# Start of a gated cross-attention kernel: second root sooner, VectorE scaling, x turned among V's products, K's first products in place of six warming ones

## What is computed

```python
h = _layernorm(x)                                 # over the 512 columns
x1 = h * rsqrt(mean(h * h) + EPS) * ln_weight
q, k, v = x1 @ w_q.T, ctx @ w_k.T, ctx @ w_v.T    # 32 heads of 128
score = softmax(where(m, q @ k + position_bias, -inf))
x = x + tanh(g_xattn) * (h + (score @ v) @ w_out.T)
x = x + tanh(g_ffn) * ffn(_layernorm(x))          # 28 experts of rank 8, the best 2
```

## Time and profile before

| | before |
|---|---|
| median of 3 runs | 825.04 us (824.33 to 826.55) |
| the profiled execution | 824.99 us, span 823.2 us |
| PE | 812.8 us busy (99%) |
| DVE | 592.9 us (72%) |
| ACT | 389.3 us (47%) |
| POOL | 454.0 us (55%) |
| mean granted clock | 0.998 |

### The profile page before, as it was taken

One profiled execution on the slowest core, in us unless ns is written; L12 is line 12 of the kernel. 1 busy time (PEld: TensorE's weight loads), 2 busy tenths in 40 slices (PEclk: granted clock), 3 DMA queues, 4 the chain that ended last, 5 costly groups with the idle time before them and its releaser, 6 DMA issues.

```text
span 823.2 us, 14190 instructions
## 1 busy us (share of the span) xinstructions
PE 812.8 (99%) x4198; PEld 694.3 (84%) x4198; DVE 592.9 (72%) x1003; ACT 389.3 (47%) x1059; POOL 454.0 (55%) x418
## 2 busy tenths in 40 slices
PE   9979999999999999999999999999999999999998
PEld 8868888887878888888888888888888888888887
DVE  6796556766775445996888778877887788778752
ACT  6954444445222424565445634563555355545410
POOL 2465666666388383757754575457545754574200
PEclk9999999999999999999999999999999999999999
DMA  9457545454543835797566556655665565555002
GB/s 319 142 182 254 174 155 165 153 162 158 179 179 116 293 129 179 236 259 264 161 211 227 180 165 213 219 180 165 219 210 182 166 226 207 179 184 179 1 27 77
DMA packets 79102, 149.70 MB, mean 182 GB/s; under 512 B 8032, under 2 KB 42336, under 8 KB 77024
## 3 DMA queue, kind: packets, MB, share of 16 engines
q1 hardware_dynamic: 79072, 149.32, 54.4%
HBM read 97.91 MB, written 51.38 MB: 181 GB/s over the span
## 4 chain that ended last, share of the span: by engine, by line
PE 91%; DVE 4%; ACT 2%; POOL 1%; DMA 1%; issue 1%; SPq 0%; DVEq 0%; POOLq 0%; ACTq 0%
PE proj_ps L2075 18%; PE proj_ps L1895 13%; PE proj_ps L2137 11%; PE proj_ps L2156 8%; PE score_ps L1895 6%; PE proj_ps L1945 5%; PE score_ps L2156 4%; PE score_ps L1914 3%; PE proj_ps L2341 2%; PE pv_ps L2137 2%; PE turn_ps L2137 2%; PE pv_ps L2156 2%; PE turn_ps L2156 2%; PE pv_ps L1914 2%; PE turn_ps L1914 2%; PE score_ps L1945 1%
## 5 line engine op out<-in xcount | busy, mean ns | idle before, releaser
L664 POOL TENSOR_TENSOR comb<-mask_add,bias_sb 128x1024 f32<-128x1024 f32 x32 | 78.3, 2468 | 145.1 <-DVE attn L1642 145.1
L906 ACT ACTIVATE attn<-attn,neg_max 128x128 f32<-128x128 f32 x256 | 99.2, 390 | 37.8 <-DVE neg_max L1631 37.7
L1161 ACT ACTIVATE w_hi<-w_raw 128x256 fp32r<-128x256 f32 x105 | 40.0, 413 | 100.1 <-POOL w_raw L755 75.2
L765 POOL TENSOR_TENSOR w_lo<-w_raw,w_hi 128x256 fp32r<-128x256 f32 x105 | 74.4, 751 | 1.8 <-ACT w_hi L1161 1.8
L1664 DVE TENSOR_TENSOR acc<-proj_ps,acc 128x512 f32<-128x512 f32 x70 | 48.1, 689 | 35.6 <-PE proj_ps L1895 35.6
L717 POOL TENSOR_TENSOR w_lo<-w_raw,w_hi 128x256 fp32r<-128x256 f32 x64 | 49.9, 783 | 25.1 <-ACT w_hi L1021 24.9
L1895 PE MATMUL proj_ps<-w_hi,tf_hi 128*128 128x512 f32 x156 | 61.1, 392 | 0.0
L1895 PE MATMUL proj_ps<-w_hi,tf_lo 128*128 128x512 f32 x156 | 60.7, 389 | 0.0
L1895 PE MATMUL proj_ps<-w_lo,tf_hi 128*128 128x512 f32 x156 | 60.7, 389 | 0.0
L660 POOL TENSOR_TENSOR w_lo<-w_raw,w_hi 128x1024 fp32r<-128x1024 f32 x19 | 45.7, 2410 | 16.1 <-ACT w_hi L892 16.1
L1457 DVE TENSOR_TENSOR w_lo<-w_raw,w_hi 128x256 fp32r<-128x256 f32 x48 | 35.2, 738 | 24.5 <-ACT w_hi L1016 24.1
(11 more groups left out here) (414 smaller groups left out, 2526.9 us busy)
## 6 DMA issues: line engine op xcount, KB each, us to landing
w_raw<-in_weights SPq DMA_DIRECT2D x50, 512.0 KB, 5.6
q_spill<-attn SPq DMA_DIRECT2D x64, 256.0 KB, 3.1
qt<-q_spill SPq DMA_DIRECT2D x16, 1024.0 KB, 4.8
v_sb<-v_spill SPq DMA_DIRECT2D x32, 512.0 KB, 3.8
block_spill<-block_sb SPq DMA_DIRECT2D x30, 512.0 KB, 3.5
attn<-block_spill SPq DMA_DIRECT2D x120, 128.0 KB, 3.0
w_raw<-in_v_weights SPq DMA_DIRECT2D x18, 512.0 KB, 4.4
v_spill<-v_sb SPq DMA_DIRECT2D x16, 512.0 KB, 4.8
```

The lines of the kernel that those rows point to most:

```text
L664: pool.tensor_tensor(comb[:, j, :, :], mask_add[:, :, :], bias_sb[:, j:j + 1, :].to_broadcast([P, B, S]), ALU.add).then_inc(comb_done, 1)
L765: pool.tensor_tensor(columns(w_lo, slot, n), raw, columns(w_hi, slot, n).bitcast(F32), ALU.subtract).then_inc(k_lo, 1)
L906: e = act.activation(probs[:, u, i, :], probs[:, u, i, :], ACT.Exp, bias=neg_max[:, u, i:i + 1], accum_out=row_sum[:, u, i:i + 1])
```

## The change

Seven places are edited. GpSimd makes the second inverse root ahead of the remainder of V's third block, and VectorE its variances ahead of the second half of the context's remainders. The layer norm of sequences 4 to 7 is applied by VectorE (a tensor_scalar with root and shift) instead of ScalarE. TensorE turns x's tiles 4 and 5 after two tiles of V's third block, and 6 and 7 after the other two. The six warming products behind the waits are gone, and K's first products stand there. In ScalarE's and VectorE's queues the splits of A, S and T are put in another order; t_raw[2] goes behind two remainders of A and two of T. GpSimd's first sums for Q's second phase wait for the third T remainder instead of Q's first product. The first context remainder moves behind Q's phases, and in V's group 1 a form is built before the last sums of group 0.

```diff
@@ gpsimd
             inverse_root(1, slice(0, G), 2)
-            pool.wait_ge(shift_done, 1)
+            inverse_root(2, slice(G, B), 2)
             early_rest(2)
-            inverse_root(2, slice(G, B), 2)
             pool.wait_ge(shift_done, 2)
             early_rest(3)
...
                 if isinstance(i, int) and i == 0:
-                    pool.wait_ge(q_prod, 1)
+                    pool.wait_ge(t_lo_done, 3)
...
-            pool.wait_ge(kt_hi_done, 1)
-            pool.tensor_tensor(kt_form_at(1, 0), kt_raw[0], kt_form_at(0, 0).bitcast(F32), ALU.subtract).then_inc(kt_lo_done, 1)
             q_phase(NQ - 2)
...
                 pool.tensor_tensor(v_raw(g, R21), v_raw(g, R22), v_raw(g, R11), ALU.subtract).then_inc(v_sums, 1)
                 if g < VE:
+                    v_last_sums(g - 1)
+                if g < VE:
                     pool.wait_ge(vw_in[R12], 16 * (g + 1))
...
+            rest_kt(0, 1)
             rest_kt(1, 2)
...
                 v_rest(g, 1)
-                v_last_sums(g - 1)
+                if g >= VE:
+                    v_last_sums(g - 1)
@@ scalar
-            layer(4)
-            layer(5)
+            raw_xt(0)
+            raw_xt(1)
             early_copy(2, 0)
-            raw_xt(0)
-            layer(6)
-            raw_xt(1)
-            early_copy(2, 1)
-            layer(7)
             raw_xt(2)
             raw_xt(3)
+            early_copy(2, 1)
+            lead_xt(4)
+            lead_xt(5)
             early_copy(2, 2)
             early_copy(2, 3)
-            lead_xt(4)
-            lead_xt(5)
...
             lead_a(0, 0, 0, 0)
+            lead_xt(6)
+            lead_xt(7)
+            early_copy(3, 0)
+            early_copy(3, 1)
+            lead_t(0)
+            lead_s(0, 0)
+            lead_s(0, 1)
+            lead_s(0, 3)
+            lead_s(0, 2)
             lead_a(0, 1, 0, 1)
             lead_a(0, 2, 1, 1)
-            lead_xt(6)
-            act.wait_ge(ve_prod, 2 * VTILES)
-            lead_s(0, 0)
-            lead_xt(7)
-            lead_t(0)
-            lead_s(0, 1)
-            early_copy(3, 0)
-            early_copy(3, 1)
             lead_t(1)
-            lead_s(0, 3)
-            lead_s(0, 2)
-            act.wait_ge(proj_done, UNITS)
             lead_t(3)
             early_copy(3, 2)
             early_copy(3, 3)
-            act.wait_ge(ve_prod, 4 * VTILES)
             lead_t(2)
@@ vector
             layer_shift(1, first)
+            x_variances(1)
             rest_ctx(0, 1)
             rest_ctx(1, 1)
             dve.wait_ge(small_in, 48)
             norm_x(0)
-            norm_x(1)
             rest_ctx(2, 1)
             rest_ctx(3, 1)
-            norm_x(2)
-            norm_x(3)
-            x_variances(1)
             layer_shift(2, second)
-            for i in range(G):
+            for i in range(1, G):
+                norm_x(i)
+            dve.wait_ge(shift_done, 2)
+            for i in range(G, B):
+                dve.tensor_scalar(acc[:, i, :], acc[:, i, :], root[:, 0, i:i + 1], shift[:, i:i + 1], ALU.mult, ALU.add).then_inc(acc_done, 1)
+            for i in range(0, G, 2):
                 rest_xt(i, xt_hi_done, xt_lo_done, xn_ps)
-            for i in range(G, B):
-                norm_x(i)
+                rest_xt(i + 1, xt_hi_done, xt_lo_done, xn_ps)
+                norm_x(G + i)
+                norm_x(G + i + 1)
...
             rest_a(0, 0, 0, 0)
-            rest_a(0, 1, 0, 1)
-            rest_a(0, 2, 1, 1)
...
             dve.tensor_tensor(t_raw[3], xt_raw[:, 2:4, half(0)], t_raw[1], ALU.subtract).then_inc(t_done, 1)
-            dve.tensor_tensor(t_raw[2], t_raw[1], xt_raw[:, 0:2, half(0)], ALU.subtract).then_inc(t_done, 1)
+            rest_a(0, 1, 0, 1)
+            rest_a(0, 2, 1, 1)
             rest_t(3, 3)
             rest_t(1, 2)
+            dve.tensor_tensor(t_raw[2], t_raw[1], xt_raw[:, 0:2, half(0)], ALU.subtract).then_inc(t_done, 1)
@@ tensor
-            pe.wait_ge(wk_part_in[0], 16)
-            for _ in range(4):
-                pe.matmul(score_ps[0][:, 0:P], ident[:, :], ident[:, :], start=True, stop=True)
-            pe.wait_ge(wk_part_lo, 1)
-            for _ in range(2):
-                pe.matmul(score_ps[0][:, 0:P], ident[:, :], ident[:, :], start=True, stop=True)
             first_keys(0)
...
-            for m in range(VTILES):
-                early_tile(2, m)
+            early_tile(2, 0)
+            early_tile(2, 1)
             turn_xn(4)
             turn_xn(5)
-            pe.wait_ge(ve_lo, 3)
-            early_tile(3, 0)
+            early_tile(2, 2)
+            early_tile(2, 3)
             turn_xn(6)
             turn_xn(7)
-            for m in range(1, VTILES):
+            pe.wait_ge(ve_lo, 3)
+            for m in range(VTILES):
                 early_tile(3, m)
```

More of the change, by code:

```diff
@@ L967, in layer @@
             def layer(i):
-                act.wait_ge(shift_done, i // G + 1)
+                act.wait_ge(shift_done, 1)
                 act.activation(acc[:, i, :], acc[:, i, :], ACT.Identity, bias=shift[:, i:i + 1], scale=root[:, 0, i:i + 1]).then_inc(acc_done, 1)
```

## The result

The changed kernel takes 827.75 us (median of 8 runs, 826.94 to 829.79) against 825.29 us before (8 runs, 824.33 to 826.55, same chip): a ratio of 1.003, 95% interval 1.0018 to 1.0042, or 2.5 us more. The forecast was 828.4, with 825.0 to 831.0 as range.

What follows compares the result with a forecast made beforehand. TensorE's waits were taken as the bound, Q's third product hanging on VectorE's queue. Terms: 4.8 at Q's third product, -1.1 near 237, -0.3 near 192, sum +3.4 on 825.04, so 828.4 us; range 825.0 to 831.0.

Steps and rivals of the forecast that it cites:

- TensorE passes K's second half unbroken: Sign against the forecast: no TensorE wait in K's second half, where about 2 us was expected at its third piece.
- What bounds the kernel: TensorE's waits are paid in full; at Q's start the third product hangs on VectorE's t_raw[2], through ScalarE's lead and copy.
- The start: K's first half, warming products removed: ends at 12.5 instead of 13.2, 0.7 us gained that buys nothing by itself.
- The second root: Root ahead of GpSimd's remainder: second shift 2.6 us sooner, but port waits and a new 2.0 us wait in K.
- A norm waits for GpSimd: VectorE's norm_x, reading two SBUF tiles, waits for GpSimd's remainder of V; taken as 2.2 us, bounds 0 and 2.2.
- the root holds no port: Rival: GpSimd's root does not block VectorE, so rest_ctx(1) and all behind come 1.5 us sooner; 827.1 us, chance 0.20.
- wait of 2.0 us at K's third piece: In K's second half, TensorE's third piece waits for rest_ctx(2) and starts at 28.4 instead of 26.2.
- The scaling: VectorE's four tensor_scalar replace ScalarE's layer(): 0.42 us each, 1.4 in all; T's first difference at 40.5 instead of 39.63.
- x among V's products: ScalarE copies V's tiles (3,0) and (3,1) before lead_t(0), so rest_t(0) starts at 46.3 instead of 45.17, +1.1 us.
- T's order: VectorE's queue before Q: two rest_a, rest_t(3) and rest_t(1) ahead of t_raw[2] make it +4.0 us later, ending at 54.9.
- The clock: Rival: clock falls after waits at 26 to 33 us and stays low longer at Q; 829.9 to 831, chance 0.13.
- Later: Form ahead of last sums near 237 gives -1.1 us; context remainder moved behind Q's phases, near 192, gives -0.3.

Runs made afterwards that it cites:

- e1_t2_back: Changed kernel with t_raw[2] again directly behind t_raw[3] in VectorE's queue; 824.32 us against 825.0 for the kernel before.
- e10_scalar_swap: Changed kernel with ScalarE's lead_t(2) behind the copies of Q's first two products; 824.28 us against 825.03 for the kernel before.
- e2_no_warming_alone: Kernel before without the six warming products, nothing else; 824.78 us against 825.0.
- e6_second_root_alone: Kernel before with only the second root and its variances sooner, second shift behind the context's remainders, ScalarE still scaling; 826.99 us against 825.75.
- e12_root_and_scaling: Kernel before with both the sooner second root and VectorE's scaling, nothing else of the change; 825.87 us against 825.03.
- e14_first_sum_ahead: e8_best_attempt with VectorE's sum of the fifth product ahead of two rest_a in Q's first phase; 820.22 us against 825.03 for the kernel before.
- e9_t2_late_alone: Kernel before with only t_raw[2] moved behind rest_t(3) and rest_t(1) in VectorE's queue; 829.35 us against 825.75.
- e4_remainder_later: Changed kernel with GpSimd's remainder of V's fourth block waiting for the seventh norm, not the second shift; 826.36 us against 825.0 for the kernel before.
- e5_scaling_alone: Kernel before with only VectorE scaling x 4 to 7 in place of ScalarE; 828.07 us against 825.75.
- e8_best_attempt: Changed kernel with the edits of e1_t2_back and e4_remainder_later, and lead_t(0) ahead of V's (3,1) copy; 822.32 us against 825.75 for the kernel before.
- e15_both: e14_first_sum_ahead with ScalarE's lead_t(2) behind the copies of Q's first two products; 821.13 us against 825.03 for the kernel before.

## Why the prediction was right, step by step

The forecast was 0.65 us above the median and its steps can be read one by one; three of them missed, and the misses nearly cancel. That the number came so near is in part luck. By one of the prediction's own signs (TensorE passes K's second half unbroken) the forecast was wrong: TensorE did pass it unbroken, from 23.79 to 29.25 us. The path behind the loss, t_raw[2] through lead_t(2) and the copy, is right.

**What bounds the kernel**: right. Q's third product hangs on t_raw[2] through lead_t(2) and the copy (e1_t2_back, e10_scalar_swap).

**The start**: half right. The edit bought nothing, as taken. But TensorE came out of K's first half at 12.91 instead of the 12.5 forecast (13.17 before), with waits of 0.19 and 0.49 us for VectorE's remainders and a slow first row. That K's first rows can run at 0.43 us without the warming ones (nine did in e2_no_warming_alone) was in no term.

**The second root**: half right. A norm waits for GpSimd as taken (4.18 us for three norms where 2.07 are free, so 2.1 for 2.2). The root does not hold the port, where I had charged 1.65 for it: this is the rival "the root holds no port". It had all behind 1.5 sooner (and 827.1, by its own numbers 826.9); T's first difference came at 39.71 instead of the 40.5 of the sum, 0.8 sooner. The wait of 2.0 us at K's third piece did not come in the kernel after. It did in four others, 1.1 to 1.4 us near 27 us: e6_second_root_alone, e10_scalar_swap, e12_root_and_scaling and e14_first_sum_ahead. In these four VectorE stood idle just before norm_x(0) (1.05, 0.69, 0.82 and 0.56 us) for the DMA of the gates. Where that lands late, GpSimd's remainder starts before the third context remainder, which then waits for it, itself or through a norm ahead of it; in the kernel after the context's remainder started at 24.18 and GpSimd's at 24.45. So this wait hangs on a landing and on a root that holds nothing; that a context remainder would wait for GpSimd's was argued rightly, which one, and that it would always be so, was not.

**The scaling**: four instructions 0.46 us apart against the 0.42 taken.

**x among V's products**: rest_t(0) at 45.49, +0.3 us instead of +1.1. This is the term that was mis-sized. TensorE reached V's last tiles sooner than in the sum, since it passed K's second half without the wait of 2.0 us: ScalarE's copy of V's tile (3,1) ended at 44.5 instead of 45.3, and lead_t(0) at 45.5 instead of 46.3. The root that held nothing stands behind that.

**T's order**: +4.0 taken. From rest_t(0)'s start to t_raw[2]'s end it is 45.49 to 54.08, 8.6 us, against 4.6: +4.0 measured. The 0.5 for GpSimd's later sums came as taken too: t_raw[2] took 1.21 us, and 1.74 in e9_t2_late_alone, where those sums ran beside it. Q's third product: +4.03 instead of +4.8.

**The clock**: named as a rival, in the sum with nothing. It should have been in the sum. After the wait of 6.5 us twelve rows of TensorE follow each other at 0.43 us instead of 0.23; before, after the pair of 2.3 us, seven did. Of the kernel before, then after:

```profile
56.12 0.40 PE L2075 MATMUL proj_ps<-tf_hi,w_hi 128*128 128x512 f32 x1
```

```profile
61.04 0.39 PE L2068 MATMUL proj_ps<-tf_hi,w_hi 128*128 128x512 f32 x1
```

Each is the 13th row from the restart: 4.35 us behind 51.77, and 5.24 behind 55.80. So +0.9 us, inside the "up to 1.1" of the rival. But this is of one execution and not a price of the wait's length: in e4_remainder_later TensorE waited the same 6.48 us, and its 13th row came 4.56 us behind the restart, 0.2 more than before:

```profile
58.46 0.39 PE L2068 MATMUL proj_ps<-tf_hi,w_hi 128*128 128x512 f32 x1
```

There the clock had fallen earlier inside the wait, so that more of the low stretch passed idle: the granted clock was 0.85 over 48 to 52 us and 0.50 over 52 to 56, with the restart at 53.90. The changed kernel had 1.00 and 0.77 there, with the restart at 55.80. The other half of the rival, a fall after the waits near 30 us, did not come in the kernel after; in e5_scaling_alone it did, behind a wait of 2.7 us at 40 (0.64 over 40 to 44).

**Later**: −1.4 taken. From that 13th row to the mark it is 274.16 us before and 272.30 after, −1.86; alone the edits gave −1.60 at the mark. The place near 192 gave 0.63 of it (TensorE's rows there stand 4.91 us behind those of before ahead of the wait, at 196.85 against 191.94, and 4.28 behind it, at 198.44 against 194.16) and the place at 237 the other 1.2. For the first the prediction took the listing's 0.3, though for the second it had itself put the real gap above the listing's.

The sum as measured: 4.03 + 0.9 − 1.86 = 3.07, and the mark says 3.06. I had 4.8 − 1.4 = 3.4. The root's term was 0.8 too high, the clock's 0.9 too low in this execution, the later one 0.5 too small. The median is 2.5 up; the 0.6 between it and the mark is within what single executions differ by.

What I had not forecast is that the loss has a cheap cure. That the third product waits for a copy behind lead_t(2) stands in the prediction's first paragraph; that the copy could go first, since T3 is needed only four products later, follows from the same lines and was not drawn.

## What to carry to other kernels

Where a wait ends with a copy in an in-order queue, look at what stands ahead of that copy and when its result is really needed: moving one entry in ScalarE's queue here took back some 3 us, a part of it the clock's, which the new order of VectorE's had lost. Edits that move work between engines should be costed as a set: the sooner root and VectorE's scaling cost 1.2 and 2.3 us alone and less than 1 together, and the later edits hid 1.9 us of the loss of the rest. When single traces are compared, take the clock's part out first: it was up to 2.4 us here, more than most of the edits. And after each repair read the waits again, since the next queue in line is seldom far behind (1.39 us here, of which moving one sum won 1.1).

## What the runs showed of the hardware

- A GpSimd power of 128x8 let VectorE's instructions with two SBUF inputs run beside it at their usual 0.6 to 0.74 us, and took 2.0 us itself instead of 1.65; a GpSimd subtraction of 128x1024 (2.4 us alone) made a scalar_tensor_tensor wait 2.1 us, and by the rows of one kernel a tensor_scalar with a single fp32 tile too (2.73 us instead of 0.54).
- The mean granted clock was below 1 in every run of the kernel before (0.996 to 0.998) and 0.994 to 0.996 in those of e9_t2_late_alone; in the traces of both it fell at the waits around Q's start. In all 18 runs of e8_best_attempt, e14_first_sum_ahead and e15_both, whose longest wait is 1.5 us, the mean was 1.000. Seven rows at half clock cost some 1.4 us, so this is a part of what those kernels won. In between the length of the wait does not settle it: e12_root_and_scaling (waits of 1.14 and 2.33 us) came out at 1.000 in 7 of its 12 runs, e10_scalar_swap (1.78 and 2.07) in 6 of 12, e1_t2_back (2.73) in 2 of 11. Nor does it settle how many rows are slow: a wait of 6.48 us was followed by 12 in one trace and 8 in another. What decides there stays open.
- Without the six warming products nine of K's first rows ran 0.43 us apart in one trace, and none to four in those of seven other kernels.
- The same DMA (block_spill) took 4.8 to 7.0 us in different traces of kernels that do not touch it, and TensorE waited up to 1.7 us for it.
